# The last layer's experts: a region of scratch for each expert, and scatters placed behind the layer norm of later batches

## The reference, cut to what matters

```
def _L3_ffn_ref(x, Wr, W1, W2):          # x: layer norm of the stream
    flat = x.reshape(-1, D)              # 4096 tokens x 256
    logits = flat @ Wr                   # 8 experts
    top_vals, top_idx = jax.lax.top_k(logits, 2)
    weights = jax.nn.softmax(top_vals, axis=-1)
    top1, w_top1 = top_idx[:, 0], weights[:, 0]
    h = gelu(einsum('td,edh->teh', flat, W1), approximate=False)
    y = einsum('teh,ehd->ted', h, W2)
    out = w_top1[:, None] * take(y, top1)
x = x + tanh(g_ffn[3]) * _L3_ffn_ref(_layernorm(x), ...)
```

## Time and profile before

| | |
|---|---|
| runs | 3241.1 us median of three (3234.79 to 3247.35) |
| profiled execution | 3239.63 us, of which its span (first to last instruction) 3237.6 us |
| busy share of the span | PE 90%, DVE 53%, ACT 37%, POOL 15% |
| last stage, from its first DVE instruction to the end | 2839.4 us to 3237.6 us |
| of that, layer norm and logits | 2839.4 us to 2883 us |
| routing on DVE | 2883 us to 2897 us |
| scatters | 2897 us to 2937 us |
| first expert matmul | 2942.8 us |

### The profile page before, as it was taken

One profiled execution on the slowest core, in us unless ns is written; L12 is line 12 of the kernel. 1 busy time (PEld: TensorE's weight loads), 2 busy tenths in 40 slices (PEclk: granted clock), 3 DMA queues, 4 the chain that ended last, 5 costly groups with the idle time before them and its releaser, 6 DMA issues. The chain is left out here.

```text
span 3237.6 us, 57916 instructions
## 1 busy us (share of the span) xinstructions
PE 2912.3 (90%) x20755; PEld 2290.6 (71%) x20756; DVE 1708.5 (53%) x4488; ACT 1192.2 (37%) x2245; POOL 496.8 (15%) x787
## 2 busy tenths in 40 slices
PE   7969999999997998998978869999799989956998
PEld 6846666666664887886855546666588877756998
DVE  4536777777773111776764457777322237741111
ACT  1315555555553121443224424454433223321221
POOL 1101111111110000000454411111000011032111
PEclk9979999999997999998879979999899999957999
DMA  3010000000001442001123320000111100064553
GB/s 116 0 33 2 1 0 0 0 0 0 0 0 53 147 151 93 19 16 57 48 91 113 97 67 21 19 19 7 61 52 52 52 18 0 0 217 138 179 178 135
DMA packets 109919, 182.36 MB, mean 56 GB/s; under 512 B 17004, under 2 KB 82668, under 8 KB 103408
## 3 DMA queue, kind: packets, MB, share of 16 engines
q1 hardware_dynamic: 99920, 155.55, 14.8%
q0 software_dynamic: 9888, 25.38, 2.2%
HBM read 149.14 MB, written 33.59 MB: 56 GB/s over the span
## 5 line engine op out<-in xcount | busy, mean ns | idle before, releaser
L507 DVE TENSOR_REDUCE m0hnm<-banks 128x4 f32<-128x1024 f32 x256 | 313.1, 1223 | 172.6 <-PE banks L435 172.5
L534 ACT ACTIVATE m0hpT<-banks 128x1024 f32<-128x1024 f32 x256 | 263.1, 1028 | 355.0 <-PE banks L448 355.0
L435 PE MATMUL banks<-m0hk,m0hq 32*128 32x256 f32 x2048 | 292.7, 403 | 12.1 <-DVE m0hnm L507 11.6
L448 PE MATMUL banks<-m0hq,m0hk 32*128 32x256 f32 x2048 | 291.8, 402 | 1.1 <-ACT m0hpT L534 1.1
L532 ACT ACTIVATE a2hpT<-banks,a2hlow 128x512 f32<-128x512 f32 x256 | 162.2, 684 | 190.8 <-PE banks L448 190.8
L435 PEld LDWEIGHTS banks<-m0hk,m0hq 32*128 32x128 f32 x2048 | 175.9, 185 | 64.0 <-DVE m0hnm L507 33.2
L507 DVE TENSOR_REDUCE a2hnm<-banks 128x4 f32<-128x1024 f32 x128 | 156.7, 1224 | 87.6 <-PE banks L435 87.6
L448 PEld LDWEIGHTS banks<-m0hq,m0hk 32*128 32x128 f32 x2048 | 177.8, 185 | 2.1 <-issue 1.7
L435 PE MATMUL banks<-a2hk,a2hq 32*128 32x256 f32 x1024 | 147.8, 406 | 21.9 <-DVE a2hnm L507 21.8
L2971 PEld LDWEIGHTS banks<-E3xT,E3w 128*128 128x128 f32 x1248 | 146.8, 194 | 3.9 <-issue 1.5
L2971 PE MATMUL banks<-E3xT,E3w 128*128 128x128 f32 x1248 | 148.4, 278 | 0.2 <-DMA E3w<-in_L_ffn_W_dram 0.2
(11 more groups left out here) (468 smaller groups left out, 6382.6 us busy)
## 6 DMA issues: line engine op xcount, KB each, us to landing
E3w<-in_L_ffn_W_dram SPq DMA_DIRECT2D x47, 1024.0 KB, 5.1
E0w<-in_L_ffn_fw_dram SPq DMA_DIRECT2D x64, 512.0 KB, 4.2
E2w<-in_L_ffn_w_dram SPq DMA_DIRECT2D x16, 1024.0 KB, 7.3
E1xin<-slots SPq DMA_DIRECT2D x71, 130.0 KB, 2.1
A2routed<-routed SPq DMA_DIRECT2D x16, 512.0 KB, 3.5
slots_x<-E3zeros SPq DMA_DIRECT2D x1, 5070.0 KB, 24.3
E3xin<-slots_x SPq DMA_DIRECT2D x39, 130.0 KB, 2.1
ctx_in<-in_ctx_dram SPq DMA_DIRECT2D x16, 256.0 KB, 4.8
```

The costliest lines, as they stand in the source:

```text
L435: ins = pe.matmul(self.scores[:, j, tc], self.q[strip(half, j), u, e, c, chunk(tc)], self.k[strip(half, j), u, e, c], start=True, stop=True)
L448: ins = pe.matmul(self.turned[:, j, kc], self.k[strip(half, j), u2, e2, c2, chunk(kc)], self.q[strip(half, j), u2, e2, c2], start=True, st ...
L507: v.tensor_reduce(self.nm[:, e, :, at:at + 33:32].rearrange("p c g -> p g c"), self.scores, AX.X, ALU.max, negate=True).then_inc(self.nm_r ...
L534: ins = a.activation(dst, self.turned, ACT.Exp)
```

## The change

The scratch gets a fixed region of 4096 + 128 rows for each expert and one dummy tile, so that a slot is the expert's base plus the token's rank in it. Ranks are made for groups of four batches: `route(g)` and `place(g)` on DVE, `ranks(g)` on PE (nine matmuls; `run` carries the counts of the groups before). `route(g)` stands behind `normalised(4g+5)`, `place(g)` behind `normalised(4g+6)`, `ranks(g)` behind `logits(4g+5)`; those of group 3 stand after the loops. ACT makes the rows of batch b-7 (`rows_of`) right after it has copied the turned batch b (`rows_turned`). POOL scatters batch b-7 right after the root of b. The 5 MB of zeros go; in their place SP writes one tile of padding behind each expert's rows (eight DMAs at register addresses) once the totals are known, and `load_x` reads each tile's address from a new table `base`.

```diff
@@ -2653,24 +2653,31 @@
     RING, XR, YR = 16, 6, 4
+    CAP = B * S + T
+    TAB = 40
+    GB = 4
+    GN = GB * C
...
+        LAG = GB + 3
+        logit_bank = lambda g: env.ps[:, 2 + 3 * (g % 2), 0:GN * E]
+        rank_bank, total_bank = env.ps[:, 3, 0:GN * E], env.ps[:, 4, 0:E]
...
-            sp.wait_ge(made, 4)
-            sp.dma_start(slots_x.rearrange("(p n) d -> p n d", p=P),
-                         zeros[:].broadcast_to([P, TILES * T // P, ROW])).then_inc(zero_in, 16)
+            sp.wait_ge(made, 5)
+            sp.dma_start(slots_x[E * CAP:E * CAP + T], pad[:]).then_inc(dummy_in, 16)
...
             def load_x(n):
+                at = sp.value_load(base[0:1, n:n + 1], min_val=0, max_val=E * CAP)
                 if n >= XR:
                     sp.wait_ge(y_used, n - XR + 1 + 2)
-                sp.dma_start(xin[:, n % XR], slots_x[n * T:(n + 1) * T]).then_inc(x_in[n % XR], 16)
+                sp.dma_start(xin[:, n % XR], slots_x[bass.ds(at, T)]).then_inc(x_in[n % XR], 16)
+
+            sp.wait_ge(tail_rdy, 1)
+            for e in range(E):
+                at = sp.value_load(tail[0:1, e:e + 1], min_val=0, max_val=E * CAP - T)
+                sp.dma_start(slots_x[bass.ds(at, T)], pad[:]).then_inc(fill_in, 16)
             sp.wait_ge(owner_rdy, 1)
             load_w1(0)
             load_w1(1)
+            sp.wait_ge(dummy_in, 16)
+            sp.wait_ge(fill_in, 16 * E)
...
-            for b in range(B):
+            g.memset(run[:, 0], 0.0).then_inc(made, 1)
+            g.memset(pad[:, 0:D + 3], 0.0).then_inc(made, 1)
+            g.memset(pad[:, D + 3:ROW], float(B * S)).then_inc(made, 1)
+            g.wait_ge(made, 5)
+
+            def root(b):
                 g.wait_ge(mv_rdy, b + 1)
                 g.tensor_tensor(side[:, C * b:C * b + C, 1], mv[:, C * b:C * b + C, 1], eps[:], ALU.add).then_inc(g_ch, 1)
                 g.wait_ge(g_ch, b + 1)
                 g.tensor_tensor(side[:, C * b:C * b + C, 1], side[:, C * b:C * b + C, 1], env.mhalf[:, 0:C], ALU.pow)\
                     .then_inc(rstd_rdy, 1)
-            g.wait_ge(zero_in, 16)
-            g.wait_ge(slot_rdy, 1)
-            for n in range(N):
-                g.wait_ge(row_rdy, n + 1)
-                g.indirect_dma_start(slots_x, bass.IndirectOffsetOnAxis(ap=slot[:, n:n + 1], axis=0), ring[:, n % RING], None)\
-                    .then_inc(sent[n % RING], 16)
+            def scatter(b):
+                if b % GB == 0:
+                    g.wait_ge(slot_rdy, b // GB + 1)
+                for n in range(C * b, C * b + C):
+                    g.wait_ge(row_rdy, n + 1)
+                    g.indirect_dma_start(slots_x, bass.IndirectOffsetOnAxis(ap=slot[:, n:n + 1], axis=0), ring[:, n % RING],
+                                         None).then_inc(sent[n % RING], 16)
+
+            for b in range(B):
+                root(b)
+                if b >= LAG:
+                    scatter(b - LAG)
+            for b in range(B - LAG, B):
+                scatter(b)
...
+            def route(g):
+                here = slice(GN * g, GN * g + GN)
+                v.wait_ge(lg_mm, GB * g + GB)
+                ch.link(v.tensor_copy(lg[:], logit_bank(g).rearrange("p (n e) -> p n e", e=E)))
+                v.sem_inc(lg_used, 1)
+                ch.link(v.tensor_reduce(m1[:], lg[:], AX.X, ALU.max))
+                ch.link(v.tensor_tensor(eq[:], lg[:], wide(m1), ALU.is_equal))
+
...
+                ch.link(v.scalar_tensor_tensor(pos[:], count[:, 0:E].unsqueeze(1).broadcast_to([P, GN, E]), float(E), eq[:],
+                                               ALU.subtract, ALU.mult))
+                ch.link(v.tensor_reduce(m2[:], pos[:], AX.X, ALU.min))
+                if g >= 1:
+                    v.wait_ge(rank_mm, g)
+                v.tensor_tensor(hot[:], pos[:], wide(m2), ALU.is_equal).then_inc(hot_rdy, 1)
+                v.wait_ge(hot_rdy, g + 1)
+
+                v.tensor_reduce(add[:], hot[:].rearrange("p n e -> p e n"), AX.X, ALU.add)
+                ch.link(v.scalar_tensor_tensor(eq[:], hot[:], -2.0 ** 126, lg[:], ALU.mult, ALU.add))
+                ch.link(v.tensor_reduce(m2[:], eq[:], AX.X, ALU.max))
+                if g >= 1:
+                    v.wait_ge(ex_rdy, g)
+                v.tensor_tensor(run[:, 1 - g % 2], run[:, g % 2], add[:], ALU.add)
+                v.tensor_tensor(m2[:], m2[:], m1[:], ALU.subtract).then_inc(gap_rdy, 1)
+
+                v.tensor_copy(side[:, here, 0], mv[:, here, 0])
+                v.tensor_copy(side[:, here, 3], token[:, here])
+
+            def place(g):
+                here = slice(GN * g, GN * g + GN)
+                v.wait_ge(rank_mm, g + 1)
+                ch.link(v.tensor_tensor(pos[:], rank_bank.rearrange("p (n e) -> p n e", e=E),
+                                        ecap[:].unsqueeze(1).broadcast_to([P, GN, E]), ALU.add))
+                ch.link(v.tensor_tensor(pos[:], pos[:], hot[:], ALU.mult))
+                ch.link(v.tensor_reduce(posf[:], pos[:], AX.X, ALU.add))
+                v.tensor_copy(slot[:, here], posf[:]).then_inc(slot_rdy, 1)
+                v.wait_ge(ex_rdy, g + 1)
+                ch.link(v.tensor_scalar(wt[:], wt[:], 1.0, None, ALU.add))
+                ch.link(v.reciprocal(wt[:], wt[:]))
+                v.tensor_scalar(side[:, here, 2], wt[:], env.tg[:, 7:8], None, ALU.mult).then_inc(side_rdy, 1)
...
@@ -2790,64 +2860,38 @@
                     moments(b - 1)
                 if b >= 2:
                     normalised(b - 2)
-            v.wait_ge(w_in, 16 * 5)
-            v.tensor_copy(side[:, :, 0], mv[:, :, 0])
-            v.tensor_copy(side[:, :, 3], token[:])
-
-            v.wait_ge(lg_mm, B)
-            ch.link(v.tensor_copy(lg[:], env.ps[:, 2, 0:N * E].rearrange("p (n e) -> p n e", e=E)))
...
-            v.wait_ge(rank_mm, 1)
-            counts = lambda j: env.ps[:, j, 0:N * E].rearrange("p (n e) -> p n e", e=E)
-            ch.link(v.tensor_copy(scan[:, 0], counts(4)))
-            v.tensor_copy(before[:], counts(3))
-            k, s = 0, 1
-            while s < N:
-                v.tensor_copy(scan[:, 1 - k, 0:s], scan[:, k, 0:s])
-                ch.link(v.tensor_tensor(scan[:, 1 - k, s:N], scan[:, k, s:N], scan[:, k, 0:N - s], ALU.add))
-                k, s = 1 - k, 2 * s
-            total = scan[:, k, N - 1]
-
...
+                if b == 2:
+                    v.wait_ge(w_in, 16 * 5)
+                    v.tensor_scalar(ecap[:], count[:, 0:E], float(CAP), None, ALU.mult).then_inc(made, 1)
+                    v.wait_ge(made, 6)
+                if b >= 2 + GB and (b - 2) % GB == 1:
+                    route((b - 2) // GB - 1)
+                if b >= 2 + GB and (b - 2) % GB == 2:
+                    place((b - 2) // GB - 1)
+            route(B // GB - 1)
+            place(B // GB - 1)
+
+
+            v.wait_ge(tot_mm, 1)
+            ch.link(v.tensor_copy(total[:], total_bank))
+            v.tensor_tensor(tail[:], total[:], ecap[:], ALU.add).then_inc(tail_rdy, 1)
...
+            v.tensor_tensor(skipped[:], past[:], tiles[:].unsqueeze(1).broadcast_to([P, TAB, E]), ALU.mult)
...
+            ch.link(v.tensor_reduce(begun[:], skipped[:], AX.X, ALU.add))
+            ch.link(v.tensor_tensor(begun[:], count[:], begun[:], ALU.subtract))
+            v.tensor_scalar(base[:], base_f[:], float(E * CAP), None, ALU.min).then_inc(owner_rdy, 1)
...
-            for b in range(B):
+            def rows_turned(b):
                 a.wait_ge(xl_mm, b + 1)
                 if b >= 2:
                     a.wait_ge(lg_mm, b - 1)
...
-            for n in range(RING):
-                row(n)
-            a.wait_ge(gap_rdy, 1)
-            a.activation(wt[:], m2[:], ACT.Exp).then_inc(ex_rdy, 1)
-            a.wait_ge(side_rdy, 1)
-            for n in range(N):
-                if n >= RING:
+            def weigh(g):
+                a.wait_ge(gap_rdy, g + 1)
+                if g >= 1:
+                    a.wait_ge(side_rdy, g)
+                a.activation(wt[:], m2[:], ACT.Exp).then_inc(ex_rdy, 1)
+
+            def rows_of(b):
+                if b % GB == 0:
+                    a.wait_ge(side_rdy, b // GB + 1)
+                for n in range(C * b, C * b + C):
                     row(n)
-                aside(n)
+                    aside(n)
+
+            for b in range(B):
+                rows_turned(b)
+                if b >= GB and b % GB == 2:
+                    weigh(b // GB - 1)
+                if b >= LAG:
+                    rows_of(b - LAG)
+            for b in range(B - LAG, B):
+                if b == B - GB:
+                    weigh(B // GB - 1)
+                rows_of(b)
...
-                        last = pe.matmul(env.ps[:, 2, n * E:n * E + E], xl[:, b % 2, k, chunk(tc)], wr[:, k],
+                        last = pe.matmul(logit_bank(b // GB)[:, n * E:n * E + E], xl[:, b % 2, k, chunk(tc)], wr[:, k],
...
+            def ranks(g):
+                pe.wait_ge(hot_rdy, g + 1)
```

(24 more changed lines are left out.)

72 lines of the change are left out of this document (28 added, 44 removed).

## The result

The changed kernel takes 3273.8 us (median of five, 3268.71 to 3280.45), the kernel before 3243.8 beside it; the ratio is 1.0098, 95% interval 1.0075 to 1.0121: slower, by 30 us in the medians and 32 by the ratio, where 18.6 were forecast. The profiled execution has a span of 3272.1 us against 3237.6.

The account below looks back on a forecast made before the run. PE at half clock was taken to bound the layer norm. Layer norm with logits 49.5 us longer, then 31 shorter to the experts, loop unchanged: 18.6 later, 3260 us; own range 3255 to 3265, widened to 3248 to 3272.

Parts of the forecast that it names:

- the circle: Layer norm: root, normalised, turn, copy, rows, scatters, next root form one chain; 6.6 us per batch against 2.45 before.
- The group steps: Layer norm: ranks on PE and place on DVE stretch a group's step to 10.15 us, 9.15 for group 2.
- PE's clock: Layer norm: PE's granted clock stays 0.50, with PE about half idle; 1.0 there would prove the forecast wrong.
- rival B: PE at full clock in the layer norm: some 20 us less than forecast, 3240; chance 7%.
- The last scatters: POOL's eight scatters left behind the routing: the last starts at 2949.7 and its completion reaches SP at 2952.4.
- SP's eight padding DMAs: Behind the totals on SP: eight register-addressed DMAs at 1.28 us each, so the first W1 is issued at 2951.3.
- Rows behind the two W1: SP's queue: first tile's rows queue behind two W1 loads and land some 8.4 us after the first W1's issue.
- To the first expert matmul: From the first tile's rows landing to the first expert matmul: 1.74 us, giving 2961.4.
- The expert loop: Expert stretch: keeps its 276 us, since load_x reads its address ahead of its wait; a 1.28 us step per tile.
- Rival C: The circle plus 0.9 waits, last scatters and W1 slowing each other, or late expert tiles: over +24, 3266 to 3280; 12%.
- expert tiles late: Expert stretch: one of three causes named for a total over +24 us; no size of its own.
- the 0.9 us waits: Layer norm: ACT's side values to the scatter taking 0.9 us throughout, not 0.30, making a turn 7.2 us.

Follow-up runs that it names:

- x9: Changed kernel with SP's eight padding DMAs moved behind the waits for all scatters, the first two W1 loads ahead of them: 3273.3 us, 1.0097 to before.
- x1: Changed kernel with each pair of scatters one root later on POOL (batch b-8 behind the root of b): 3241.0 us, 1.0014 to before.
- x2: Changed kernel with SP loading the first two W1 ahead of the eight padding DMAs: ratio 1.0089 to the kernel before.
- x3: Kernel before with only the tiles' row loads at register addresses read from a table: ratio 1.0028 to before, loop 294.5 us.
- x4: Kernel before with only the scratch declared at the changed kernel's 33920 rows: ratio 0.9996 to before, loop 284.0 us.
- x5: Changed kernel with SP issuing the row load of tile n+3, not n+4, behind W1 of tile n: 3268.0 us, loop 283.7.
- x8: Changed kernel with roots ahead of scatters, later group steps, row loads one place later, prefix-sum ranks, half the padding on ACT's queue: 3229.0 us, 0.9955 to before.
- x7: Changed kernel with all roots ahead of scatters, group routing and placing later, loop row loads one place later: 3235.3 us, 0.9977 to before.

## Why the prediction was wrong

The direction and the circle were right, the time, 3260 with a range to 3272, was not: 3273.8. By its steps, times counted from the first `normalised` (2842.17 before, 2843.55 in the changed kernel):

- **The circle: right.** 6.6 us a turn was forecast; the six steps without a group's work were 7.18, 6.59, 6.59, 7.06, 6.58, 6.59. ACT's side values to the scatter was 2880.17 - 2879.89 = 0.28, against 0.30.
- **The group steps: 0.5 high.** 9.52, 9.55 and 8.72 against 10.15, 10.15 and 9.15. The batches before them took 16.7 against 16.1, and the turns behind a group 0.5 more than the others. That the last `normalised` came after 85.1 us, exactly as forecast, is partly luck: +0.6, +1.0 and -1.7 us cancel.
- **PE's clock: 0.50 throughout**, against rival B, with PE busy 57% of the stretch in place of 89%.
- **The last scatters: right.** The last one starts after 108.0 us, against 107.5.
- **SP's eight padding DMAs: the first step that failed.** They were sized by layer 1's 1.28 us each, first W1 after 109.1 us; it was 116.9, 7.8 more, because SP's instructions came 0.70 us apart beside the scatters. The neighbours of the row were not the fault. Layer 1's padding in before, 1677.08 to 1686.4, stood beside scatters all the way too:

```profile
1681.18 0.96 POOL L1599 DMA_INDIRECT slots<-E1rows,E1slot  x1 [0.30 <-issue]
...
1686.24 0.96 POOL L1599 DMA_INDIRECT slots<-E1rows,E1slot  x1 [0.30 <-issue]
```

  The price came from one execution in which SP was not slowed (9.0 us from first to last issue); in the changed kernel's own profile the same layer 1 padding took 13.4. x9 shows that the slow steps need scatters in flight, x1 and x2 that scatters in flight don't always bring them. What else it takes stays open, and the trace of before couldn't have told it.
- **Rows behind the two W1: right.** 8.4 us from the first W1's issue to the rows was forecast, 7.8 measured (2960.49 to 2968.25); the rows landed 4.89 us after their own issue, where alone they take 2.1, and 2.04 in x9, with W1 long in. By the Trainium skill, page DMA: Bandwidth & Descriptors, section Queues, rings and completion order, SP's DMAs share one row of rings, and each DMA engine takes their descriptors in ring order, so that rows queue behind the W1 issued before them: the trace agrees.
- **To the first expert matmul: 1.74 us, as before.**
- **The expert loop: the second step that failed.** "The expert loop keeps its 276 us: load_x reads its address ahead of its wait" looked at SP's time per tile and not at who stands behind it. This was also one of the prediction's own signs of being wrong ("if the expert loop differs from 276 us by more than 2"). W1 was issued 5.40 us before its use and took 5.1 at the median; 0.2 us at SP and 0.4 at the landing turned an unseen slack of 0.3 us into 7.2 over 39 tiles. x3 shows that the register address alone does it, x4 that the scratch doesn't, x5 that W1's place in SP's order does.

18.6 forecast, 7.2 for the padding (7.8, less the 0.6 by which the rows landed sooner behind W1) and 7.2 in the loop make 33.0, which is what the profile has, and the ratio says 32. Rival C held the sign and size of what happened (over +24), and of its three causes "expert tiles late" was a part; the 0.9 us waits never came. Its third cause, the last scatters and W1 slowing each other, is absent in the changed kernel, whose first W1 goes out 9 us after the last scatter started, but it came wherever a W1 pair stood beside scatters: x1 and x2, and in before itself, where the scatters at 2898.31 and 2899.58 took 6.1 and 6.5 us to land.

The gain that the change was after is real: scatters did leave the tail. x1 shows what the order of two lines on POOL cost, x8 that with the other repairs the same idea beats the kernel before by 0.4%.

## What to carry to other kernels

When an in-order engine gets work from another stage placed between its own steps, follow the chain back from what it waits for: if it passes through the result that this engine must make next, move the foreign work one place later. Before an instruction is added to a queue, find the load that stands behind it and compare its lead with its landing; a slack of 0.3 us doesn't show as a wait in the profile. Take a price from more than one execution before a sum rests on it: eight padding DMAs beside scatters cost 9 us in the trace that the price came from, and 16 in later ones.

## What the runs showed of the hardware that was not expected

- SP's instructions, 0.02 to 0.3 us apart otherwise, came 0.70 us apart while GpSimd's indirect DMAs were in flight: the last layer's eight register-addressed DMAs took 16 to 19 us in place of 8 to 9. Two sessions of the experiments and the changed kernel's first profile showed it, one session in none of its four profiles, and a share in it of the recording is not excluded. ACT's queue did not escape it: of the four padding DMAs that it issued in x8 beside scatters, the first two came 1.15 us apart, and the last two took from 2910.56 to 2916.24.
- A scatter of 128 rows issued while two 1 MB loads began on another queue landed 6.1 us after its start in x1 and 6.5 to 7.3 in x2; without them 2.4 to 2.7.
- A 128x260 row load with its address in a register was issued 0.17 us after its wait ended, with a fixed address 0.02, though the address had been read before the wait; and the 1 MB load behind it landed at a median of 5.5 us, against 5.1.
- PE's granted clock was 0.50 through the layer norm with PE busy 57% of it in the changed kernel, 89% in before and 92% in x7.
